# Ending the attention block at its last head sums, and running its last norms beside the expert weight splits

## The reference

```python
x = L0_attn_x                                   # 4 x 512 x 128
xn = _layernorm(_layernorm(x), ln1_g, ln1_b)
q = xn @ Wq; k, v = split(xn @ Wkv)             # 16 heads of 64, one k and v
attn = softmax(q k^T * 64 ** -0.5)              # 512 x 512 for each head
x = x + _layernorm((attn @ v) @ Wo, ln2_g, ln2_b)
h = _layernorm(x)
probs = softmax(h @ gate_w.T)                   # 8 experts
topw, sel = top_k(probs, 2); topw /= topw.sum()
gu = h @ gate_up_w[e].T                         # 2 x 512 for each chosen expert
hact = gu[512:] * gelu(gu[:512])
x = x + sum over chosen e of topw[e] * (hact @ down_w[e].T)
```

## Time and profile before

| what | value |
|---|---|
| median of 3 runs | 663.44 us (662.64 to 664.55) |
| profiled execution, its own time | 664.06 us |
| span of the profile | 662.3 us |
| busy share PE, DVE, ACT, POOL | 88%, 65%, 46%, 57% |
| mean granted TensorE clock | 0.941 of full speed |

### The profile page before, as it was taken

The page is one execution under the profiler, slowest core; times in us unless marked ns, Lnnn a source line. Parts: engine busy times, 40 slices in busy tenths (PEclk is TensorE's granted clock), DMA queues, the critical chain, the costliest instruction groups (busy, mean ns, idle before and its releaser), DMA issues. The chain is left out here.

```text
span 662.3 us, 8662 instructions
## 1 busy us (share of the span) xinstructions
PE 581.3 (88%) x2569; PEld 329.3 (50%) x2569; DVE 431.8 (65%) x792; ACT 307.7 (46%) x578; POOL 379.6 (57%) x315
## 2 busy tenths in 40 slices
PE   2799999999999998899999899999760995999990
PEld 1354554444544543455444344443320783888880
DVE  2876668569658686965777696569868462444433
ACT  3245655456465542545554344654215731555540
POOL 4347766577669664985975588693515144333330
PEclk9889999999999996999999799999875897999996
DMA  5111101011010000320000000000008111310005
GB/s 166 65 66 65 52 15 66 0 66 66 0 66 33 33 1 1 131 94 0 1 1 1 0 18 17 1 0 1 21 12 223 42 30 40 82 42 22 23 14 190
DMA packets 23981, 29.29 MB, mean 44 GB/s; under 512 B 4403, under 2 KB 14901, under 8 KB 23936
## 3 DMA queue, kind: packets, MB, share of 16 engines
q1 hardware_dynamic: 21664, 24.50, 11.3%
q0 software_dynamic: 2272, 4.24, 2.0%
HBM read 13.73 MB, written 15.32 MB: 44 GB/s over the span
## 5 line engine op out<-in xcount | busy, mean ns | idle before, releaser
L899 ACT ACTIVATE prob<-s_ps 128x512 f32<-128x512 f32 x256 | 150.8, 598 | 193.7 <-PE s_ps L1008 191.7
L805 DVE TENSOR_REDUCE rowmax<-max_ps 128x1 f32<-128x512 f32 x256 | 173.5, 686 | 91.4 <-PE max_ps L977 88.6
L744 POOL TENSOR_TENSOR fold<-prob 128x1024 f32<-128x1024 f32 x61 | 144.9, 2376 | 104.4 <-ACT prob L899 103.8
L1022 PE MATMUL pv_ps<-prob,v 128*64 128x512 f32 x512 | 141.1, 631 | 0.0
L1006 PE MATMUL s_ps<-q_hl,khh 128*128 128x512 f32 x256 | 119.0, 465 | 1.6 <-DMA q_hm<-mrow 1.1
L977 PE MATMUL max_ps<-khh,q_hl 128*128 128x512 f32 x256 | 105.8, 421 | 8.6 <-DVE q_hl L794 4.4
L1008 PE MATMUL s_ps<-q_hm,kly 65*128 65x512 f32 x256 | 103.1, 403 | 0.0
L1006 PEld LDWEIGHTS s_ps<-q_hl,khh 128*128 128x128 f32 x256 | 49.0, 192 | 81.4 <-ACT prob L899 57.2
L1173 POOL DMA_INDIRECT parts<-eow,xs x39 | 38.2, 980 | 84.0 <-DVE eow L1221 83.1
L750 POOL TENSOR_TENSOR psums<-fold 128x512 f32<-128x512 f32 x61 | 78.9, 1294 | 4.8
L977 PEld LDWEIGHTS max_ps<-khh,q_hl 128*128 128x128 f32 x256 | 50.6, 198 | 29.5 <-DVE rowmax L805 10.0
(11 more groups left out here) (194 smaller groups left out, 771.4 us busy)
## 6 DMA issues: line engine op xcount, KB each, us to landing
sorted_rows<-blank SPq DMA_DIRECT2D x36, 260.0 KB, 2.6
raw_w<-in_gate_upT SPq DMA_DIRECT2D x7, 512.0 KB, 4.7
xs<-sorted_rows SPq DMA_DIRECT2D x39, 65.0 KB, 1.9
wd<-in_downT SPq DMA_DIRECT2D x8, 256.0 KB, 5.5
xs<-parts SPq DMA_DIRECT2D x8, 256.0 KB, 4.5
x<-in_x SPq DMA_DIRECT2D x4, 256.0 KB, 5.4
out<-x SPq DMA_DIRECT2D x4, 256.0 KB, 2.3
parts<-eow,xs POOLq DMA_INDIRECT x39, 2.3
```

Source lines behind the costliest of these rows:

```text
L744: nc.gpsimd.tensor_tensor(fold[:, :, :], prob[:, head % 4, 0:2, :], prob[:, head % 4, 2:4, :], ALU.add).then_inc(prob_folded, 1)
L805: nc.vector.tensor_reduce(rowmax[:, group % 2, it, i:i + 1], max_ps[:, k % 2, :], AX_X, ALU.max).then_inc(max_done, 1)
L899: nc.scalar.activation(prob[:, head % 4, jt, :], s_ps[:, k % 2, :], ACT.Exp, scale=SCALE).then_inc(exp_done, 1)
L1022: last = nc.tensor.matmul(pv_ps[DH * hd:DH * hd + DH, :], v[:, b % 2, jt, :], prob[:, head % 4, jt, :], start=(jt == 0), stop=(jt == JT - 1))
```

## The change

- `psums`, `raw`, `ao`, `rinv`, `wof` and four PSUM banks become tensors of the whole program, and the steps RAW, RECIP, RSPLIT, NORM and OUT become functions (`tail_vector`, `tail_scalar`, `tail_tensor`) that both blocks call. All of those that stand behind the last PV step are taken out of block 1 and issued in block 2.
- The second half of the last unit's SUM gets a bank of its own. NORM 0 and 1 of the last unit, OUT 0 and 1 and everything later move behind that SUM, in the order of `LAST_STEPS`. Block 1 ends with PV and SUM.
- `VECTOR_HEADS` keeps only head 7; POOL adds up heads 3 and 5 as it does the others. Head 7's sum on DVE is three additions of 128x512, each behind one EXP step, in place of one reduction.
- `LATE_AFTER_AT` places CHOOSE3 and what follows one to three slots earlier.
- In block 2 ACT makes RAW and then all eight `wh` and `x_high(0)` ahead of `yT`. POOL makes the low parts of experts 0 to 3 in pieces of 128x512, DVE those of 4 to 7: three behind the attention's last steps, one behind YSTAT.
- XSTAT moves in between the tiles, XNORM to CHOOSE4 and RANK one tile later.
- PE loads the experts of the first 17 tiles behind OUT 1, all at once, followed by `turn_in(0)`; then come NORM 2, NORM 3, OUT 2, OUT 3. Before, each tile loaded its own.
- On POOL each row DMA waits for a tile's weighted result (`eow_ready` of k-2). SP no longer waits for the low weights, as the raw weight of expert 7 and the rows no longer share memory.

```diff
@@ -86,15 +86,13 @@
                 place(after + NORM_AT[c] + OUT_LAG, 5, "OUT", u, c)
         else:
 
-            for half, start in enumerate((after + HALF_AT[0], after + HALF_AT[1])):
-                place(start, 6, "SUM", u, half)
-                for c in range(4):
-                    place(start + 1 + c, 6, "RECIP", u, 4 * half + c)
-                place(start + 5, 6, "RSPLIT", u, half)
-                for c in range(2):
-                    pair = 2 * half + c
-                    place(start + 6 + c, 8, "NORM", u, pair)
-                    place(max(start + 8 + c, after + HALF_AT[1]), 9, "OUT", u, pair)
+            for c, at in enumerate(HALF_AT):
+                place(after + at, 6, "SUM", u, c)
+            for c in range(4):
+                place(after + HALF_AT[0] + 1 + c, 6, "RECIP", u, c)
+            place(after + HALF_AT[0] + 5, 6, "RSPLIT", u, 0)
+            for n, (kind, a) in enumerate(LAST_STEPS):
+                place(after + HALF_AT[1] + 1, 9 + n, kind, u, a)
     return [step for _, _, step in sorted(placed, key=lambda entry: entry[:2])]
 
...
 
-LATE_AFTER_AT = (29, 30, 33, 41, 45, 47, 48, 48, 49, 50, 52, 54, 56, 57, 59, 61, 62, 63)
+LATE_AFTER_AT = (29, 30, 33, 41, 45, 47, 48, 48, 49, 50, 52, 53, 54, 55, 56, 58, 59, 60)
...
 SUM_AT = (-7, 5)
 
-HALF_AT = (-9, 0)
+HALF_AT = (-9, 4)
+
+
+LAST_STEPS = (("NORM", 0), ("RECIP", 4), ("NORM", 1), ("OUT", 0), ("RECIP", 5), ("RECIP", 6), ("RECIP", 7), ("OUT", 1),
+              ("RSPLIT", 1), ("NORM", 2), ("NORM", 3), ("OUT", 2), ("OUT", 3))
 
 FIRST_Q_AT = (-3, 3)
...
 
-VECTOR_HEADS = (3, 5, 7)
+VECTOR_HEADS = (7,)
...
+        last_pv = max(n for n, step in enumerate(steps) if step[0] == "PV")
+        tail_steps = [step for step in steps[last_pv:] if step[0] in ("RAW", "RECIP", "RSPLIT", "NORM", "OUT")]
+        assert all(step in tail_steps or step[0] in ("PV", "SUM") for step in steps[last_pv:])
+        steps = [step for step in steps if step not in tail_steps]
...
+                    if kind == "EXP" and a % JT >= 1 and vector_sums(u * UH + a // JT):
+
+                        head, jt = u * UH + a // JT, a % JT
+                        total = psums[:, head % SUM_SLOTS, :]
+                        if jt == 1:
+                            dve.wait_ge(sum_mm, (head - SUM_SLOTS) // 4 + 1)
+                        dve.wait_ge(exp_done, head * JT + jt + 1)
+                        added = nc.vector.tensor_tensor(total, prob[:, head % 4, 0, :] if jt == 1 else total,
+                                                        prob[:, head % 4, jt, :], ALU.add)
+                        if jt < JT - 1:
+                            link(dve, added)
+                        else:
+                            added.then_inc(vec_sum, 1)
+                    tail_vector(dve, kind, u, a)
...
-            BETWEEN = {"XNORM": 0, "X3T": 1, "LOGIT": 2, "CHOOSE0": 2, "CHOOSE1": 3, "CHOOSE2": 3, "CHOOSE3": 4, "CHOOSE4": 4, "CHOOSE5": 5,
-                       "RANK": 5, "PLACE": 6, "LIST0": 7, "LIST1": 8, "LIST2": 9}
+            BETWEEN = {"XSTAT": 1, "XNORM": 2, "X3T": 3, "LOGIT": 3, "CHOOSE0": 3, "CHOOSE1": 4, "CHOOSE2": 4, "CHOOSE3": 5,
+                       "CHOOSE4": 5, "RANK": 6, "CHOOSE5": 6, "PLACE": 6, "LIST0": 7, "LIST1": 8, "LIST2": 9}
             BEFORE = [kind for kind in AFTER_STEPS if kind not in BETWEEN]
...
+            POOL_LOW = (0, 1, 2, 3)
+            VECTOR_LOW = tuple(e for e in range(E) if e not in POOL_LOW)
+
+            def low_gate_up(eng, e, done, pieces=1):
+
+
+                eng.wait_ge(wh_ready, e + 1)
+                for n in range(pieces):
+                    part = slice(n * GU // pieces, (n + 1) * GU // pieces)
+                    cols = slice(e * GU + part.start, e * GU + part.stop)
+                    last = eng.tensor_tensor(wl[:, cols], raw_w[e][:, part], wh[:, cols].bitcast(F32), ALU.subtract)
+                last.then_inc(done, 1)
+
             def sent(eng, k):
...
-                sp.wait_ge(wl_ready, E)
...
+                for e in POOL_LOW:
+                    low_gate_up(pool, e, wl_pool, 2)
                 for kind in BEFORE:
                     after_gpsimd(pool, kind, LB)
                 for k in range(NT + 3):
                     for kind in between(k):
                         after_gpsimd(pool, kind, LB)
                     if k in ROW_SENDS:
+
+                        pool.wait_ge(eow_ready, k - 2)
                         send_rows(k - SEND_AT)
                     for tile in range(results_due(k - 1), results_due(k)):
                         send(tile)
...
+                for step in tail_steps:
+                    tail_vector(dve, *step)
+                for e in VECTOR_LOW[:3]:
+                    low_gate_up(dve, e, wl_ready)
                 for kind in BEFORE:
                     after_vector(dve, kind, LB, bank)
-                    if kind == "YSTAT":
-                        for e in range(E):
-                            low_gate_up(e)
-                        x_low(0)
+                for e in VECTOR_LOW[3:]:
+                    low_gate_up(dve, e, wl_ready)
+                x_low(0)
                 for k in range(NT + 3):
                     if 0 <= k - 3:
                         weigh(k - 3)
...
+                for step in tail_steps:
+                    if step[0] == "RAW":
+                        tail_scalar(act, *step)
+                for e in range(E):
+                    high_weights(e)
+                x_high(0)
+                for step in tail_steps:
+                    if step[0] == "OUT":
+                        tail_scalar(act, *step)
                 for kind in BEFORE:
                     after_scalar(act, kind, LB, bank)
-                    if kind == "YT":
-                        for e in range(4):
-                            high_weights(e)
-                    if kind == "YADD":
-                        for e in range(4, E):
-                            high_weights(e)
-                        x_high(0)
                 for k in range(NT + 3):
                     if k + 1 < NT:
                         x_high(k + 1)
@@ -1299,7 +1346,7 @@
                     pe.wait_ge(xs_in[k], 16)
...
+                tile_expert = []
+
+                def load_expert(k):
+
+                    tile_expert.append(pe.value_load(tile_at[0:1, 0, k:k + 1], min_val=0, max_val=E - 1))
+
+                for step in tail_steps:
+                    tail_tensor(pe, *step)
+                    if step == ("OUT", last_unit, 1):
+                        pe.wait_ge(tiles_ready, 1)
+                        for k in range(FIRST_TILES):
+                            load_expert(k)
+                        pe.wait_ge(raw_ready, UNITS * UP)
+                        turn_in(0)
                 for kind in BEFORE:
-                    step(kind)
-                turn_in(0)
-                tile_expert = []
+                    between_step(kind)
                 for k in range(NT + 2):
                     if k + 1 < NT:
                         turn_in(k + 1)
                     if k < NT:
-                        if k in (0, FIRST_TILES):
-                            pe.wait_ge(tiles_ready, 1 if k == 0 else 2)
+                        if k == FIRST_TILES:
+                            pe.wait_ge(tiles_ready, 2)
+                        if k >= FIRST_TILES:
+                            load_expert(k)
                         if k == 0:
-                            pe.wait_ge(wl_ready, E)
-                        tile_expert.append(pe.value_load(tile_at[0:1, 0, k:k + 1], min_val=0, max_val=E - 1))
+                            pe.wait_ge(wl_ready, len(VECTOR_LOW))
+                            pe.wait_ge(wl_pool, len(POOL_LOW))
                         pe.wait_ge(xel_ready, k + 1)
                         if k >= 2:
                             pe.wait_ge(gelu_done, k - 1)
@@ -1361,14 +1422,17 @@
                         if k >= 2:
                             pe.wait_ge(ha_ready, k - 1)
                         times(up_ps[:, k % 2, :], k, F).then_inc(up_mm, 1)
+                    for kind in between(k):
+                        if kind != "LOGIT":
+                            between_step(kind)
                     if 0 <= k - 1 < NT:
                         turn_hidden(k - 1)
                     if k == 2:
                         pe.wait_ge(wd_in, 16 * E)
                     if 0 <= k - 2:
                         down(k - 2)
-                    for kind in between(k):
-                        step(kind)
+                    if "LOGIT" in between(k):
+                        between_step("LOGIT")
 
 
```

More of the change, by code:

```diff
@@ new lines, in vector_sums, with sums_done @@
+        def vector_sums(head):
+            return head // UH == last_unit and head % UH in VECTOR_HEADS
+        gpsimd_heads = [h for h in range(UNITS * UH) if not vector_sums(h)]
+        vector_heads = [h for h in range(UNITS * UH) if vector_sums(h)]
+        vec_sum = sem("vec_sum")
```

(41 more changed lines are left out.)

219 lines of the change are left out of this document (86 added, 133 removed).

## The result

The changed kernel took 653.47 us (median of four, 651.19 to 654.41) against 664.0 for the kernel before beside it (also four): ratio 0.9845, interval 0.9807 to 0.9882. It is faster by 1.2 to 1.9%, 10.5 us, where 25 were forecast. The time lies in the range (633 to 654) and near rival one (652.5), but that is chance. The profiled execution took 651.19 us, the fastest of the four, 11.6 more than the sum's 639.6: 5.6 of them lie in front of the first gate, where that rival has no loss, and 5.7 in the tiles 10 to 20, where it has 13.5. Its span of 649.5 is 12.8 shorter than that of before.

A forecast was written before the change was run, and what follows sets the result against it. PE, busy 88% of the span, was taken to bound the tiles at 2.84 us each; 664.06 less 13.0 (earlier first gate) and 13.5 (stall), plus 1 and 1, gave 639.6, forecast as 639, range 633 to 654.

The forecast's parts named there:

- rival one: In the tiles, the 13.5 us stall of ACT and DVE stays, its cause being unseen; 652.5 us, chance 0.22.
- the sum's 639.6: Whole kernel: the profiled execution's 664.06 us with -13.0, -13.5, +1 and +1 applied.
- Block 2's start: End of block 1: PE's and POOL's sides end together, POOL's last, at about 480 us; bounds 478 to 487.
- the term of the 17 loads: Block 2 before NORM 2: PE's expert loads take 7.7 us and make NORM 2 3.6 late; bounds 0 to 8.
- The rest of that stretch: Block 2's start to the first gate apart from the loads: NORM, RECIP, `yT`, z, YSTAT and low parts, 17.2 us.
- So I take the stall of 13.5 as gone: Tiles 9 to 12: spreading the row DMAs removes the 13.5 us stall; bound of 0 gained.
- no wait released by something remote: Sign that the forecast is right: no such wait in tiles 7 to 14, at 2.84 us each.
- the gate of tile 12: Sign that the forecast is wrong: that gate comes over 43 us behind the gate of tile 0.
- The first ten tiles: XSTAT and POOL's residual sum between ACT's and DVE's tile steps add 1 us; bounds 0 to 4.
- Tile 17's wait: The last row DMA follows tile 11's result, so tile 17's rows come late, adding 1 us; bounds 0 to 3.
- Rival two: Block 1 ends late on POOL, or block 2's head is 4 or more longer; 643 to 647, chance 0.14.
- The slower rival: In the tiles, each paced row DMA brings a wait, eight tiles losing 44 us; 683 us, chance 0.06.

The follow-up runs named there:

- e7: The kernel of e4 with the last three row DMAs of block 1 issued in block 2, ahead of POOL's low parts; 645.2 us.
- f1: The kernel of e7 in which POOL also waits for DVE's RSPLIT ahead of its low parts; 643.2 us.
- e6: The kernel before with heads 3 and 5 of the last unit summed by POOL instead of DVE, nothing else; 660.1 us, ratio 0.9968.
- e1: The changed kernel with each of the first 17 experts loaded by PE in its own tile, as before; 646.6 us, ratio 0.9766.
- e2: The changed kernel without the wait of each row DMA for a tile's result; 659.2 us, ratio 0.9948.
- e5: The kernel before with all of POOL's DMAs paced from turn 7 on, nothing else of the change; 654.9 us, ratio 0.9873.
- e3: The changed kernel with the result DMAs paced as well, POOL waiting at every turn from 7 on; 650.2 us, ratio 0.9808.
- r2: The changed kernel, unchanged, run again in the third session; 648.1 us, ratio 0.9955.
- r1: The kernel before, unchanged, one run for its profile in the third session; 649.7 us.
- h2: The changed kernel without the pacing of its row DMAs, again, in the fourth session; 657.6 us, ratio 0.9935.
- r3: The changed kernel with experts loaded in their own tiles and result DMAs paced too, in the third session; 643.0 us, ratio 0.9869.
- e4: The changed kernel with experts loaded in their own tiles and result DMAs paced too, second session; 641.5 us, ratio 0.9863.

## Why the prediction was right and wrong

- **Block 2's start** was put at 480 and came at 480.87. That close a hit is luck: in fourteen profiles with the same block 1 program (the change and the runs made from it, without `e7` and `f1`) it lies between 476.1 and 483.6. The row DMAs started at 464.13 (465.5 predicted), and POOL's side was the later one. Two things in the working were wrong and offset each other. Their early start was put down to the two reductions alone; `e6` shows that these don't move them without the earlier slots. And the meeting behind POOL's last DMA took 2.9 us, where 0.5 was assumed.
- **The first step that failed** is the term of the 17 loads, between block 2's start and the first gate: 20.8 was predicted and 25.5 measured. I took 0.45 us a load, beginning with OUT 1's issue at 3.5 us after the start, and 3.6 us of delay for NORM 2. The array ended OUT 1 at 5.9 us, then stood for 8.98, and without the loads (`e1`) NORM 2 starts 6.4 us earlier and the first gate lies 5.5 earlier. So the term was mis-sized, 3.6 against 5.5 on the path.
- **The rest of that stretch** I had at 17.2, and `e1` shows 20.1. RSPLIT takes 2.8 us against the 1.3 of before (1.20 for the cast and 1.64 for the rest, beside POOL's low parts). Its two rows in the timeline before:

```profile
488.60 0.43 DVE L827 CAST rih<-rinv 128x512 fp32r<-128x512 f32 x1
489.06 0.75 DVE L829 SCALAR_TENSOR_TENSOR rhl<-rih,low_rows,rinv 128x512 fp32r<-128x512 f32 x1
```

From NORM 2's `ao` to `yT` it is 4.8 us (489.53 to 494.37) where I took 3.26 from before: there the granted clock was 1.00 from 490 to 496, in `e1` 0.50 from 487 to 490 and 0.60 from 490 to 495. The Trainium skill (SBUF — State Buffer, section Who interferes with whom) has the second of a DVE and a POOL instruction that exclude each other wait for the whole of the first. The trace agrees for a single fold and for the cast in the changed kernel; `e7` shows more, a cast that took 9.03 us in a row of POOL instructions. I had named this price and called POOL's low parts hidden; what they do to RSPLIT stood on the path.
- **The second step that failed** is "So I take the stall of 13.5 as gone". Measured, the stretch of tiles 10 to 20 fell by 6.8. Pacing does what it was taken to do: without it (`e2`) a stall is back, with it alone (`e5`) the kernel before gains 8.4. But only the row DMAs were paced. I wrote that the queued result DMAs do no harm, and read `results_due` as one and a half DMAs a tile; they are issued without a pause until the backlog is gone, and the stall came back there. With them paced too (`e3`) its waits are 1.7 us long at most. Of my signs, "no wait released by something remote" caught this; the gate of tile 12 did not, since the stall had moved behind it.
- **The first ten tiles** lost 2.4, in place of 1, inside the bound of 4. 0.7 of it lie in front of tile 2's transposition, which waits 0.52 us for DVE's `xel`. Tile 5's transposition follows that of tile 4 by 6.3 us: ACT waits 1.34 us for POOL's `offset` with XNORM and PE then waits 1.35 us for ACT, with `turn_hidden` and `down` queued behind. Tile 17's wait was 1.19, as said.
- **The forecast as a whole** rested on the stall being the kernel's. In sessions without it the change gives 3.0 us (`r2`), 4.2 at tile 1's transposition and 0.7 at the end, less 1.9 in the tiles. The chances named the stall's unseen cause and gave it 0.22; that half of it would move, and that another session lacks it, was in no case. Rival two's longer head of block 2 did come (4.7 us), but RSPLIT beside POOL is only 1.5 of it, and the loads, which that rival didn't name, are 1.9 beyond their term. The slower rival didn't happen: a single paced row DMA brought no such wait.

What starts the stall isn't settled. Shown: in sessions that have it, it lies in rows of seven to twelve POOL DMAs without a pause, and goes with them; behind four there is a wait of 1.3 to 2.0 us. In the third session, on the chip of the first, the same row of twelve in the same kernel does nothing (`r1`), and a row of nine in `r2` neither. What differs between sessions no view shows.

## What to carry to other kernels

Load registers from memory where the engine has queued work in front of it, one at a time, not in a row ahead of an instruction that others wait for: the version with that undone and all of POOL's DMAs paced took 641.2 to 643.0 us in three sessions, against 648.1 for the change in the one that had both. When one stream of DMAs is paced, look at what the pacing holds back, and pace its release; here that paid only in the sessions with the stall. Before a stall without a visible releaser is counted as gain, measure the kernel before again at another time.

## What the runs showed of the hardware

- Seventeen register loads in a row left the array idle for 8.98 us (the change and `r2` alike; 9.55 in `h2`), 0.53 each, while a single one shows as about 0.45: they didn't overlap each other.
- After an indirect DMA as POOL's last instruction of a block, the engines went on 2.7 to 2.9 us after its end (the change, `e1`, `r2`, `r3`); with POOL idle earlier (`e7`, `f1`), 0.4 us after PE's last one.
- A DVE cast of 0.5 us once took 9.03 and ended only behind the last of eight POOL subtractions of 128x512 without a pause (`e7`); in the same kind of row it otherwise took 1.09 to 1.34 (the change, `e1`, `e4`).
- The kernel before took 663.3 and 651.2 us on the same chip in two sessions. Of the 14.4 us between its profile of the result's session and that of the third (`r1`), 12.9 lie between the transpositions of tiles 10 and 13 (22.1 against 9.2).
